# Value products of four attention phases in two half bursts, copy and turn one slot later

## What is computed

```
qkv = x @ w_qkv                                  # 16 heads of 8
scores = einsum('bhqd,bhkd->bhqk', q * gate, k) / scale
attn = softmax(where(causal, scores, -inf), -1)
out = einsum('bhqk,bhkd->bhqd', attn, v)         # the value products
return out.transpose(0, 2, 1, 3).reshape(B, T, D) @ w_out
```

## Time and profile before

| what | value |
|---|---|
| median of 3 runs | 3533.31 us (3531.64 to 3540.31) |
| the profiled execution | 3533.18 us, its span 3530.9 us |
| TensorE busy, products | 2712.3 us (77%) |
| TensorE busy, weight loads | 1810.2 us (51%) |
| VectorE busy | 2145.8 us (61%) |
| ScalarE busy | 1307.7 us (37%) |
| GpSimd busy | 983.5 us (28%) |
| exponentials of the second attention, L569 | x512, 492 ns each |
| row maxima of the second attention, L792 | x512, 549 ns each |

### The profile page before, as it was taken

One profiled execution on the slowest core, in us unless ns is written; L12 is line 12 of the kernel. 1 busy time (PEld: TensorE's weight loads), 2 busy tenths in 40 slices (PEclk: granted clock), 3 DMA queues, 4 the chain that ended last, 5 costly groups with the idle time before them and its releaser, 6 DMA issues. The chain is left out here.

```text
span 3530.9 us, 69910 instructions
## 1 busy us (share of the span) xinstructions
PE 2712.3 (77%) x20859; PEld 1810.2 (51%) x20884; DVE 2145.8 (61%) x5390; ACT 1307.7 (37%) x2884; POOL 983.5 (28%) x1089
## 2 busy tenths in 40 slices
PE   5888624317887887679849987788879998997999
PEld 3666524305665664528725555566634474455444
DVE  5776672137888786512247775777555567846455
ACT  1566201003665565324316663356432222133221
POOL 2332106852334332265622322334200020011000
PEclk6999756557999999889959998799989999998999
DMA  3332302334433331316521110333100004400000
GB/s 74 52 49 35 129 36 53 48 77 57 54 44 49 49 46 14 145 60 127 92 68 27 24 23 7 50 46 48 38 2 1 0 6 96 96 7 25 5 0 24
DMA packets 164036, 165.85 MB, mean 47 GB/s; under 512 B 30472, under 2 KB 136720, under 8 KB 158736
## 3 DMA queue, kind: packets, MB, share of 16 engines
q1 hardware_dynamic: 128240, 138.50, 20.4%
q0 software_dynamic: 34336, 21.83, 4.4%
q10 hardware_dynamic: 1152, 1.61, 0.1%
HBM read 52.90 MB, written 33.01 MB: 24 GB/s over the span
## 5 line engine op out<-in xcount | busy, mean ns | idle before, releaser
L569 ACT ACTIVATE a1PR<-bank 128x384 f32<-128x384 f32 x512 | 242.4, 492 | 143.6 <-PE bank L626 140.7
L792 DVE TENSOR_REDUCE a1NM<-bank 128x3 f32<-128x384 f32 x512 | 263.0, 549 | 26.6 <-PE bank L608 24.6
L795 DVE TENSOR_REDUCE a2NMQ<-bank 128x2 f32<-128x512 f32 x256 | 168.1, 685 | 60.8 <-PE bank L612 60.6
L959 PE MATMUL bank<-ONES 128*128 128x256 bf16 x960 | 169.5, 283 | 26.4 <-DMA f1nWR<-in_wr 5.0
L569 ACT ACTIVATE a2PR<-bank 128x512 f32<-128x512 f32 x256 | 149.6, 596 | 91.3 <-PE bank L630 89.2
L792 DVE TENSOR_REDUCE a4NM<-bank 128x3 f32<-128x384 f32 x256 | 136.1, 552 | 57.0 <-PE bank L608 55.3
L792 DVE TENSOR_REDUCE a0NM<-bank 128x3 f32<-128x384 f32 x256 | 136.6, 553 | 50.2 <-PE bank L608 47.4
L624 PE MATMUL bank<-a1QH,a1KH 128*128 128x128 bf16 x512 | 115.6, 227 | 57.4 <-ACT a1PR L569 43.1
L569 ACT ACTIVATE a4PR<-bank 128x384 f32<-128x384 f32 x256 | 121.2, 489 | 97.5 <-PE bank L626 96.6
L569 ACT ACTIVATE a0PR<-bank 128x384 f32<-128x384 f32 x256 | 119.9, 489 | 82.7 <-PE bank L626 82.0
L2208 POOL DMA_INDIRECT routed<-yY,yID x80 | 123.6, 1545 | 85.7 <-DMA routed<-yY,yID 41.4
(11 more groups left out here) (675 smaller groups left out, 8334.9 us busy)
## 6 DMA issues: line engine op xcount, KB each, us to landing
lVB<-lV SPq DMA_DIRECT2D x64, 256.0 KB
yWT<-in_w SPq DMA_DIRECT2D x40, 256.0 KB, 3.0
a1QH<-a1SPL SPq DMA_DIRECT2D x96, 64.0 KB
a1KH<-a1SPL SPq DMA_DIRECT2D x96, 64.0 KB
a1QH<-a1QH SPq DMA_DIRECT2D x96, 64.0 KB
a1KH<-a1KH SPq DMA_DIRECT2D x96, 64.0 KB
rows_by_slot<-gZB SPq DMA_DIRECT2D x5, 1040.0 KB
yXG<-rows_by_slot SPq DMA_DIRECT2D x40, 130.0 KB, 3.1
```

The source lines that it names most:

```text
L569: nc.scalar.activation(PR[:, h % 8, :], bank[2 + h % 2][:, 0:NC], ACT.Exp, scale=SCALE)\
L792: v.tensor_reduce(NM3[:, h, :], S_BANK[h % 3][:, 0:NC].rearrange("p (n k) -> p n k", n=3), AX, ALU.max, negate=True).then_inc(s_used.sem, 1)
L795: v.tensor_reduce(NMQ[:, :, h], S_BANK[h % 3][:, 0:NC].rearrange("p (n k) -> p n k", n=2), AX, ALU.max, negate=True).then_inc(s_used.sem, 1)
L959: pe.matmul(bank[7][:, 0:2 * P], spare[:, 0:P], spare[:, :], start=True, stop=True)
```

## The change

Each burst is cut at the keys: the four products with the first 128 keys stay in the slot h % 4 == 1, the four with the second 128 keys move to the next slot, h % 4 == 2, behind that slot's score products. The waits for the exponentials and for bank 4 stay with the first half, the semaphore that reports the burst with the second. The copy of a set on ScalarE and its turn on TensorE move one slot later, and with the turn everything that is counted from it: the scaling on VectorE, L_LAST, L_COMBINE, L_CTT, L_OUT and L_TMP.

```
-        burst_at = lambda h: ((h - 5) // 4 % NU, 0 if h >= 5 else -1) if h % 4 == 1 else None
-        copy_at = {(4 * PK * (s + 1) + 2) % NH: (s, (4 * PK * (s + 1) + 2) // NH) for s in range(NS)}
-        turn_at = {4 * PK * (s + 1) + 4: s for s in range(NS)}
+        burst_at = lambda h: ((h - 5) // 4 % NU, 0 if h >= 5 else -1, h % 4 - 1) if h % 4 in (1, 2) else None
+        copy_at = {(4 * PK * (s + 1) + 3) % NH: (s, (4 * PK * (s + 1) + 3) // NH) for s in range(NS)}
+        turn_at = {4 * PK * (s + 1) + 5: s for s in range(NS)}
...
-        L_LAST = 4 * PK * NS + 4 - NH
+        L_LAST = 4 * PK * NS + 5 - NH
...
-            def values(b, j, u):
+            def values(b, j, u, n):
                 s, a = u // PK, u % PK
-                after(pe, p_ready, b, 4 * u + 4)
-                if a == 0:
-                    after(pe, ct_ready, b, s)
-                for n in range(2):
-                    for g in range(4):
+                if n == 0:
+                    after(pe, p_ready, b, 4 * u + 4)
+                    if a == 0:
+                        after(pe, ct_ready, b, s)
+                for g in range(4):
...
-                mm.then_inc(pv_done.sem, 1)
+                if n == 1:
+                    mm.then_inc(pv_done.sem, 1)
...
-                        u, back = burst_at(h)
-                        values(t + back, (m + back) % LEAD, u)
+                        u, back, n = burst_at(h)
+                        values(t + back, (m + back) % LEAD, u, n)
```

More of the change, by code:

```diff
@@ L411, in attention_phase @@
         L_OUT, L_TMP = L_CTT + 1, L_CTT + (1 if diff else 2)
-        turned_users = [(p % NH, 0, -(p // NH), cx_ready, s + 1) for s, p in enumerate(4 * PK * (s + 1) + 4 for s in range(NS))]
+        turned_users = [(p % NH, 0, -(p // NH), cx_ready, s + 1) for s, p in enumerate(turn_at)]
         bank7_users = sorted(turned_users + [(L_OUT, 1, -1, tmp_ready, 1)]
@@ L631, in scores_t @@
                 mm.then_inc(st_ready.sem, 1)
-            def values(b, j, u):
+            def values(b, j, u, n):
                 s, a = u // PK, u % PK
-                after(pe, p_ready, b, 4 * u + 4)
-                if a == 0:
-                    after(pe, ct_ready, b, s)
-                for n in range(2):
-                    for g in range(4):
[L641 to L647, removed]
-                mm.then_inc(pv_done.sem, 1)
+                if n == 0:
[3 more added lines that the diff above has]
+                for g in range(4):
+                    p = 4 * u + g
+                    v = vslot(head(p))
+                    x = v % PK * 2
+                    w = VX[:, j, n * (SV // PK) + v // PK, x:x + 2, :].rearrange("p q x -> p (q x)")
+                    o = V_BANK[32 * g:32 * g + 32, P if n and causal else 0:T]
+                    rhs = PR[:, p % 8, n * T:min(NC, n * T + T)]
+                    mm = pe.matmul(o, w, rhs, start=(a == 0 and n == 0), stop=(a == PK - 1 and n == 1), skip_group_check=True)
+                if n == 1:
+                    mm.then_inc(pv_done.sem, 1)
             def turn(b, s):
```

## The result

The changed kernel takes 3586.7 us (median of 4 runs, 3585.2 to 3589.6) against 3533.6 us: a ratio of 1.0148 (1.0130 to 1.0165), 53 us slower. The forecast was 3547 us with a range up to 3578, so the sign was right and the size was not.

The account below looks back on a forecast made before the run. TensorE's own order and its waits were taken as the bound. From 3533.2 us, the first to fourth attentions added +3, +22, -4 and -7: 3547 us, own range 3537 to 3561, overall range 3508 to 3578.

Parts of the forecast that it names:

- The split's price: TensorE, all four attentions: entering and leaving a burst twice costs +0.20 us a burst, 64 us over 320 bursts.
- the hidden weight load: Rival: the second half's weights load ahead, hiding its entry on TensorE; 29 us less, 3518 us; chance 0.05.
- Part 3: Second attention: the chain through GpSimd plus slots 14 to 31, +1.4 us an image, +22 us, bounds 0 and 2.2.
- The chain, +0.6: Second attention: squares, sums, GpSimd's power and the awaited exponential start later, behind a fifth row maximum: +0.6 us an image.
- some 0.1 comes back where VectorE no longer stands behind GpSimd: Second attention's chain: VectorE was to be freed from standing behind GpSimd, returning some 0.1 us.
- Slots 14 to 31, +0.8: Second attention after the awaited exponential: splits and new waits less the waits lost by turns, +0.8 us an image.
- the +0.45: Second attention, slot 14: the second half burst now comes after the wait for the exponential, +0.45 us an image.
- the relief of slot 16: Second attention: the turn of slot 16 loses its wait of 0.62 us.
- the transposes of slot 18: Second attention: the maxima transposes there stand one slot behind a turn, not two, +0.6 us.
- slots 25 and 26: Second attention: ScalarE ahead of TensorE again in slot 26, -0.2 us.
- No term of the sum is a clock term.: All four attentions: granted clock 0.97 to 0.99, and the change adds TensorE work rather than pauses, so no clock cost.
- every switch on the path: Rival: relieved waits reappear one for one at L725, L736 and the exponentials, +64 us, 3597 us; chance 0.15.

Follow-up runs that it names:

- the added products: Kernel before the change plus sixteen products nothing reads, in slot 13 of the second attention: ratio 0.9979, that attention 553.2 us.
- three sets late: Against the kernel before, second attention only: halves, sixteen unread products, copy and turn one slot later for third, fourth and last set: ratio 1.0063, attention 584.8 us.
- the two filled kernels: Kernel before and changed kernel, each with sixteen unread products in slot 13 of the second attention: ratios 0.9979 and 1.0145.
- later transposes: Changed kernel with sixteen unread products, second attention's maxima transposes one slot later (19 and 31): ratio 1.0070, that attention 589.2 us.
- move in three: Kernel before with whole bursts, copy and turn one slot later in first, third and fourth attention only: 3550.5 us, ratio 1.0043.
- the sums first: Kernel before with the change in the fourth attention; in the second, VectorE takes scaling and sums of squares ahead of the row maxima: ratio 0.9983.

## Why the prediction was wrong, and where it was right

**Right, in part by luck.** The bound was TensorE's own order, and the four terms were read stage by stage. The split's price was 0.24 us a burst (0.20). Each wait that was to go went, and those that were to take its place are in the lists: L726 on L584, the transposes on the scaled context. First and fourth came to +3.3 and -4.4 (forecast +3 and -7), which is within the scatter of single profiles; the fourth also spent 7.3 us less at the 1.2 GHz level. Their steady images tell it better: from the seventh to the twelfth, all at the full clock, they average 16.4 us before and 16.5 after in the first, 18.59 and 18.30 in the third, 17.05 and 16.86 in the fourth, so +0.1, -0.29 and -0.19, where +0.18, -0.25 and -0.42 were forecast. The sums were near; their terms don't hold one by one. Where the forecast has 0.80 for the halves, they cost 0.6 and 0.5 alone in these images of the first and fourth; the move, -0.6 and -1.2 by its terms, gave 0.0 and +0.1 alone, and -0.5 and -0.7 on top of the halves. In the third the move alone brings the whole -0.29. Of the rivals the hidden weight load is out: the second half starts 0.15 us after the score product ahead of it.

**Wrong: the second attention's +1.4 us an image (Part 3).** From the last section the 60.6 us are made up one after the other, each step the difference of two profiles: the added products -3.2 (556.4 to 553.2), the halves +7.0 (to 560.2), three sets late +24.6 (to 584.8), the other five +18.3 (to 603.1), and the clock +13.9 (to 617.0). Single profiles carry a few us of scatter each, the filled ones among them still spend 20 to 36 us at the 1.2 GHz level, and another order of the steps would share them out differently. By the prediction's own steps:
- *The chain, +0.6.* Measured +1.2 us an image. The step that failed is "some 0.1 comes back where VectorE no longer stands behind GpSimd". It stands behind it again, earlier in the scaling, with two more steps to follow, and the maxima behind them come 0.78 us later. The fifth maximum was priced rightly at 0.5, and the 0.2 for the square was not there.
- *Slots 14 to 31, +0.8.* At the full clock (the two filled kernels) the image is 38.0 - 34.5 = 3.4 us longer, 1.2 of it ahead of slot 14, so 2.2 in these slots. From the starts of the score products, in us an image, the forecast's terms put with their slots and 0.2 for each split:

| slots | 14 | 15, 16 | 17, 18 | 20, 21 | 22 | 25, 26 | 28 to 30 |
|---|---|---|---|---|---|---|---|
| forecast | +0.45 | -0.62 | +0.8 | -0.67 | +0.8 | 0 | +0.04 |
| measured | 0.0 | 0.0 | +1.2 | -0.9 | +1.1 | +0.6 | +0.2 |

In slot 14 the +0.45 did not come, though the halves alone pay it (0.51 at the full clock). The terms that failed by costing more are the relief of slot 16, whose turn lost its wait while the output product and the context's transpose (0.52 and 0.38 us there), a slot later now, wait in its place; the transposes of slot 18; and slots 25 and 26, where I took ScalarE to be ahead again. The run with later transposes puts 1.1 us of the image down to their distance from a turn, where I had 0.6 and -0.16 for the two.
- *"No term of the sum is a clock term."* This failed in two stages. In the second attention the clock is 13.9 us. In the third the steady image is 18.59 us before and 18.30 after, a gain of 0.29 as forecast (0.25), but its first image takes 24.5 us instead of 20.2. The clock in that image, before and after:

```profile
1852.00:1858.00 6.00, 6.00 (x33) 4.11 (x35) 4.48 (x8) 3.79 (x8) 2.30 (x2) 0.50 0.10 25
1858.00:1864.00 6.00, 6.00 (x64) 3.84 (x54) 4.14 (x10) 3.04 (x6) 0.71 (x1) 0.87 0.35 50
```

```profile
1912.00:1918.00 6.00, 6.00 (x34) 2.75 (x31) 3.78 (x6) 2.97 (x6) 1.16 (x1) 0.50 0.18 41
1918.00:1924.00 6.00, 6.00 (x36) 3.74 (x33) 3.08 (x7) 2.19 (x4) 0.71 (x1) 0.50 0.26 31
```

Before, TensorE comes back to full speed 11 us behind the first score product of the stage, after, not until 20 us; 9 us at half the clock instead of the whole accounts for the 4 us. Every profile in which the third attention had the halves shows a first image of 24.4 us or more, every one with whole bursts in their old place 19.7 to 20.2 us; the move alone showed 19.5 in one profile and 23.8 in another. What keeps the clock down there was not tried by itself.

The rival "every switch on the path" had a time near the result (3597), for another reason: at the full clock only half of the second attention's switches reach the end of its shortest image.

What stays open: how the five sets other than the third, fourth and last share their 18 us, why the halves alone cost the third attention 34 us, and why the clock falls in one profile and not in another of the same instructions (the second attention of "move in three").

## What to carry to other kernels

Price a wait by what follows it, too: where TensorE already stands still for near two microseconds an image, a little more can halve its clock for several microseconds (here 2.50 us instead of 1.76), and the mean granted clock of the kernel before, 0.97, did not show it. When a step is moved by a slot, lay the order of every engine beside it again: here it fell on GpSimd's subtraction at a worse place and one slot too close to the next user of its bank. Terms of two parts of a change need not hold for each part by itself: in the first and fourth attention the move gained only on top of the halves. And a chain made shorter pays only where its wait was the last one: with the sums first, the same time was lost at a score bank and in slot 14.

## What the hardware showed that I had not expected

- Around the end of a wait of 2.50 us the granted clock fell to 0.50 for 3.4 or 6.8 us in each of the 13 images that have it; after 1.8 to 2.0 us (halves alone) in 12 of 13; at 1.76 us mostly not, though one profile of the same instructions spent 73.9 us of the attention there instead of 38.5. Sixteen products that nothing reads, put into the wait, kept it at 0.97.
- At the start of the third attention TensorE stayed at 0.50 for 20 us from its first score product although it was busy 6.00 of 6 us, with the bursts in halves; 11 us with whole ones.
- An operation of VectorE on 4 elements per partition took 0.93 us instead of 0.17 while GpSimd subtracted, and ended with it.
